# A decoder block's second stage: row transposes, router product and both halves of the routing one step later

## What is computed

```python
x = x + self_attention(layernorm(x))                 # 16 heads, ALiBi, causal
x = x + cross_attention(layernorm(x), ctx, mask)     # 8 heads of 64, 750 context rows of 384
h = layernorm(x)
scores = softmax(h @ w_router)                       # 8 experts
weights, experts = top_k(scores, 2)
slot = position of the token among those of its expert, in order of the tokens
x = x + sum_k weights[k] * expert_k(h) + bias        # 896 slots for each expert
```

## Time and profile before

| | |
|---|---|
| median of three runs | 3380.05 us |
| the profiled execution | 3391.78 us, of which 3390.1 us from the first to the last instruction |
| mean granted clock of TensorE | 0.951 |
| busy over the span | PE 91%, DVE 49%, ACT 40%, POOL 22% |
| first stage | from 0 to about 840 us |
| second stage | from about 840 to 1980 us, a batch in the loop in about 71 us |
| third stage | from about 1980 us to the end |

### The profile page before, as it was taken

One profiled execution on the slowest core, in us unless ns is written; L12 is line 12 of the kernel. 1 busy time (PEld: TensorE's weight loads), 2 busy tenths in 40 slices (PEclk: granted clock), 3 DMA queues, 4 the chain that ended last, 5 costly groups with the idle time before them and its releaser, 6 DMA issues. The chain is left out here.

```text
span 3390.1 us, 52927 instructions
## 1 busy us (share of the span) xinstructions
PE 3071.0 (91%) x19340; PEld 2500.3 (74%) x19340; DVE 1669.1 (49%) x3816; ACT 1351.4 (40%) x2297; POOL 732.2 (22%) x564
## 2 busy tenths in 40 slices
PE   5889999865999999999999839999999999999997
PEld 4667777754777777777777628887888788878886
DVE  5888888843555565555555623232223232323232
ACT  5677777743555555555555411111111111111111
POOL 0000000001112222121221123333333333333333
PEclk9889999977999999999999859999999999999999
DMA  2011111114111111111110022222222222222222
GB/s 95 23 34 44 43 43 43 44 50 145 37 37 43 36 51 52 36 37 42 48 54 23 17 70 72 61 83 70 74 61 83 70 74 63 81 72 72 66 78 59
DMA packets 96191, 193.80 MB, mean 57 GB/s; under 512 B 18656, under 2 KB 28640, under 8 KB 94016
## 3 DMA queue, kind: packets, MB, share of 16 engines
q1 hardware_dynamic: 80912, 160.78, 15.6%
q0 software_dynamic: 15152, 31.26, 4.4%
HBM read 144.19 MB, written 47.82 MB: 57 GB/s over the span
## 5 line engine op out<-in xcount | busy, mean ns | idle before, releaser
L1619 DVE CAST f_hh<-f_hf 128x448 fp32r<-128x448 f32 x256 | 116.8, 456 | 893.2 <-ACT f_hf L1643 860.5
L1643 ACT ACTIVATE f_hf<-f_h 128x448 f32<-128x448 f32 x256 | 139.6, 545 | 1016.0 <-PE f_h L1679 983.2
L1566 POOL TENSOR_TENSOR f_w1l<-f_raw,f_w1h 128x512 fp32r<-128x512 f32 x130 | 183.4, 1411 | 829.2 <-DVE f_w1h L1601 829.1
L1695 PE MATMUL f_y<-f_w2h,f_hh 128*128 128x512 f32 x896 | 357.9, 399 | 0.0
L1695 PE MATMUL f_y<-f_w2h,f_hl 128*128 128x512 f32 x896 | 354.0, 395 | 0.0
L1695 PE MATMUL f_y<-f_w2l,f_hh 128*128 128x512 f32 x896 | 352.3, 393 | 0.0
L1266 ACT ACTIVATE c_s_sb<-c_s_sb,c_nmx 112x750 f32<-112x750 f32 x256 | 236.0, 922 | 188.9 <-DVE c_nmx L1095 186.5
L1679 PE MATMUL f_h<-f_xTh,f_w1h 128*128 128x448 f32 x1024 | 261.8, 378 | 32.3 <-ACT f_hf L1643 16.8
L1258 ACT COPY c_pT<-c_psum 125x672 f32<-125x672 f32 x256 | 184.7, 722 | 241.1 <-PE c_psum L1359 237.4
L1359 PEld LDWEIGHTS c_psum<-c_ident,c_s_sb 112*125 112x125 f32 x1536 | 198.2, 194 | 90.2 <-issue 84.5
L1679 PE MATMUL f_h<-f_xTl,f_w1h 128*128 128x448 f32 x1024 | 256.1, 373 | 0.0
(11 more groups left out here) (243 smaller groups left out, 5725.5 us busy)
## 6 DMA issues: line engine op xcount, KB each, us to landing
f_raw<-in_w SPq DMA_DIRECT2D x132, 512.0 KB
c_craw<-in_ctxT SPq DMA_DIRECT2D x16, 1125.0 KB, 5.1
a_x_in<-in_x SPq DMA_DIRECT2D x9, 896.0 KB, 5.7
a_xr<-in_x SPq DMA_DIRECT2D x8, 896.0 KB, 6.0
x_dram<-a_xr SPq DMA_DIRECT2D x8, 896.0 KB, 4.8
q_dram<-a_q SPq DMA_DIRECT2D x32, 224.0 KB, 5.3
c_q<-q_dram SPq DMA_DIRECT2D x16, 448.0 KB, 5.5
c_x<-x_dram SPq DMA_DIRECT2D x16, 448.0 KB, 4.6
```

The lines of the kernel that those rows point to most:

```text
L1566: pool.tensor_tensor(w1s[1][:, n % NSLOT].rearrange("p k c -> p (k c)"), raw1[:, g % 2, n % 2, :], w1s[0][:, n % NSLOT].rearrange("p k c - ...
L1619: dve.tensor_copy(hs[0][:, l % 2, c * HC:c * HC + HC], hf[:, c, :]).then_inc(h_hi, 1)
L1643: act.activation(hf[:, c, :], H[:, 0:HC], ACT.Gelu_apprx_tanh).then_inc(free, 1)
L1695: mm = pe.matmul(Y[t][:], hs[a][:, l % 2, 128 * t:128 * t + 128], w2s[b][:, l % NSLOT, :], start=j == 0 and q == 0, stop=j == FB - 1 and q ...
```

## The change

Five things move one step on in each batch: XT(0) from step 7 to 8, XT(1) from 8 to 9, RT from 10 to 11 (in the last slot, behind K(2,0)), DVE's two halves of the routing from 11 to 12 and from 14 to 15, and ACT's small exponential from 11 to 12. PRE goes from the end of step 13 to the first slot of step 14, behind the scores and ahead of the transposes of that step. No instruction is added or taken away.

```diff
--- before.py
+++ after.py
@@ -817,9 +817,9 @@
         RT, PRE = ("RT", 0, 0), ("PRE", 0, 0)
 
         PLAN = {0: ([], [K(3, 1)], []), 1: ([], [PV(3)], [V(1, 0)]), 2: ([], [V(1, 1)], []), 3: ([], [V(1, 2), OUT(0)], []),
-                4: ([], [OUT(1)], []), 5: ([], [PV(0)], []), 6: ([], [K(0, 0)], []), 7: ([], [K(0, 1)], [XT(0)]),
-                8: ([], [K(1, 0)], [XT(1)]), 9: ([], [PV(1)], []), 10: ([], [V(0, 0)], [RT]), 11: ([K(1, 1)], [K(2, 0)], []),
-                12: ([], [V(0, 1)], []), 13: ([], [PV(2)], [PRE]), 14: ([], [V(0, 2)], []), 15: ([K(2, 1)], [K(3, 0)], [])}
+                4: ([], [OUT(1)], []), 5: ([], [PV(0)], []), 6: ([], [K(0, 0)], []), 7: ([], [K(0, 1)], []),
+                8: ([], [K(1, 0)], [XT(0)]), 9: ([], [PV(1)], [XT(1)]), 10: ([], [V(0, 0)], []), 11: ([K(1, 1)], [K(2, 0)], [RT]),
+                12: ([], [V(0, 1)], []), 13: ([], [PV(2)], []), 14: ([PRE], [V(0, 2)], []), 15: ([K(2, 1)], [K(3, 0)], [])}
         LATE = (K(3, 1), V(1, 0), V(1, 1), V(1, 2))
         START = [K(0, 0), K(0, 1), K(1, 0), K(1, 1), K(2, 0), V(0, 0), V(0, 1), V(0, 2), K(2, 1), K(3, 0)]
 
@@ -1199,9 +1199,9 @@
                     residual(i, kind, s // 4)
                 elif s == 6:
                     layernorm(i)
-                elif s == 11:
+                elif s == 12:
                     routing(i, kind, 0)
-                elif s == 14:
+                elif s == 15:
                     routing(i, kind, 1)
 
             mask_of(0)
```

## The result

The change makes the kernel slower: 3476.86 us in the median of six runs (3471.33 to 3484.63) against 3381.09 us for the kernel before on the same chips, a ratio of 1.0282 with a 95% interval of 1.0269 to 1.0295. The forecast was 3461 us and the range 3437 to 3495. Of the 95.8 us that were added, the forecast had 81.

What follows compares the result with a forecast made beforehand. PE was taken to bound the second stage, except in a stall ended by DVE's masking. Terms 5.5 + 13.7 + 46.6 - 4 = 62 us, plus 20 for the clock, made 82: 3461 us from the median of 3380.05, range 3437 to 3495.

Steps and rivals of the forecast that it cites:

- What bounds the stage: Second stage: PE is busy but for one stall of 1.23 and 0.91 us a batch, ended by DVE's masking before S(8).
- Term A: Transposes and router product: XT(0), moved out of the stall behind S(8), costs 0.39 us a batch; 5.5 us.
- Term B: Routing's first half in step 12: DVE's masking delays S(14) from +7.85 to +8.83 after S(12); 13.7 us.
- Term C: PRE and routing's second half: K(2,1) waits 3.0 us for PRE's bank; S(0) comes 3.33 us later a batch, 46.6 us.
- Rival 3: PRE's bank doesn't hold K(2,1), being given back ahead of head-half 1's masking; 20 us added, 3400 us; chance 0.07.
- Term D: PE's waits for ACT's copy, 4.3 us over the second stage, should mostly go: -4 us.
- The clock: Drops of the granted clock behind stalls: 11 at K(2,1) of 1.6 us, 2 more at step 8 of 1.2; 20 us.
- Rival 1: DVE's waits as forecast, but clock drops stay as many as they are: 62 us added, 3442 us; chance 0.22.
- Rival 2: The clock drops behind all three stalls in every batch: 113 us added, 3493 us; chance 0.12.
- The prediction's last step: Adding 82 us to the profiled 3391.8 us gave 3473 us; from the median of 3380.05 us, 3461 us.
- rival 4: Faster: the wait for the layernorm ahead of S(8), priced at 17.2 us, goes for good, 3363 us; chance 0.04.
- rival 5: Nothing that shows: the moved pieces are small and cancel, within 0.3% of 3380 us (10 us); chance 0.03.

Runs made afterwards that it cites:

- e9: As e3, with the layernorm's root left in step 6 and the scaling of the rows moved behind the masking of step 7: 3392.45 us, ratio 1.0029.
- e12: As e10, with the last three instructions of the layernorm's root also moved behind the masking, into step 7: 3356.51 us, ratio 0.9916.
- e10: As e9, with POOL's two additions on x1 held until DVE has scaled head-halves 9 and 11: 3365.52 us, ratio 0.9954.
- e5: Kernel before with only RT moved to step 11 and the routing's first half and ACT's small exponential to step 12: 3398.05 us, ratio 1.0057.
- e3: Kernel before with only XT(0) and XT(1) moved, to steps 8 and 9: 3396.40 us, ratio 1.0043.
- e2: Changed kernel with only the routing second half's first two instructions (reading PRE, giving its bank back) in step 14, the rest in 15: 3401.60 us, ratio 1.0057.
- e7: The kernel before, unchanged, run once more for a second profile: 3384.00 us, ratio 1.0003.
- e1: Changed kernel with the whole second half of the routing back in step 14: 3399.77 us, ratio 1.0053 to the kernel before.
- e6: Kernel before with only PRE moved to step 14 and the second half of the routing to step 15: 3442.15 us, ratio 1.0172.
- e11: Kernel before with only POOL's two waits of e10 added: 3378.42 us, ratio 0.9990.

## Why the prediction was right, and where it was off

- **What bounds the stage.** PE, but for DVE's masking at S(8). Right, and shown by e9 and e12, which move work from ahead of the masking to behind it and shorten S(6) to S(8) by 0.97 and 1.70 us.
- **Term A**, the transposes. Forecast 0.39 us a batch, measured 8.30 - 7.77 = 0.53 from S(8) to S(10) less 0.10 from S(10) to S(12), so 0.43. The total is near, the places were not quite right: XT(0) takes over XT(1)'s place at no cost, and it is XT(1), now behind PV(1), that costs 0.53 us (1389.49 to 1390.02 above), where I had written "nothing"; the 0.10 is saved by RT, for which I had also written "nothing". e10, which moves XT but not RT, has 8.30 in every batch and still 9.77 from S(10) to S(12); e5, which moves RT, has 9.66. That the stall itself stays is shown by e3 (S(6) to S(8) 8.86).
- **Term B**, the first half. Forecast S(12) to S(14) 8.83, measured 8.84. The chain held link by link: DVE goes on at +4.61 (1404.31 - 1399.70), forecast +4.62; the negation is at +8.74, forecast +8.81. Shown by e5.
- **Term C**, PRE and the second half. Forecast +3.33 a batch, measured 11.60 - 8.43 = 3.17 in the four batches without a drop: K(2,1) starts at +7.65 (1416.19 - 1408.54), forecast +7.75, and waits 2.87 us, forecast 3.0. That the giving back of PRE's bank and nothing else holds K(2,1) is shown by e2, where the wait goes with those two instructions alone. Rival 3 falls.
- **Term D**, the waits for ACT's copy: forecast -4 us, measured nothing: the second profile of the kernel before (e7) doesn't have them, and no other kernel's profile shows them in this place. This was the step that failed: it took a row that varies between executions of one kernel for a property of the kernel.
- **The clock.** Forecast 20 us: 11 drops at K(2,1) of 1.6 us and 2 more at S(8) of 1.2. Measured at K(2,1): 10 drops of 1.5, 15 us. At S(8): the drops take 14 x (9.96 - 8.30) = 23 us after and 14 x (8.81 - 7.77) = 15 us in e7, so 9 us more where I had 2.4. The number of drops was near (10 at either place, forecast 11); the size at S(8) wasn't. A drop there costs 1.1 us or 2.5, and I had priced one from the cheaper kind, though the profile of the kernel before has one batch with the dearer (10.34 against 7.77). That the number came near is partly luck: I had no rule for it, and a stall of the same 2.72 us has a drop behind it in 10 batches of 14 in the changed kernel, 4 in e1, 5 in e2 and 14 in e3. Rival 1, no further loss by the clock, falls. It was also what the Trainium skill's advice on idle gaps would have said ("TensorE: Matmul & The Clock Gate", section "Why this matters for your kernels"); the trace disagrees, with drops in 10 of 14 batches behind waits of 2.72 and of 2.87 us. Rival 2, a drop behind all three stalls, falls too: none in 14 follows the wait of 1.28 us.
- **Rivals 4 and 5** had 0.07 together. e3 shows what the wait for the layernorm was worth once the transposes stepped out of it: nothing. So rival 4 falls, and rival 5 by the 95.8 us.

The sum that the two profiled executions show, 6 + 14 + 44 + 0 + 24 = 88 us, is 6 above my 82 (4 at term D, 4 at the clock, and 2 less at term C). The other 8 us between 88 and 96 are the distance of those executions from their medians. The prediction's last step is also 1 us low: 3391.8 + 82 is 3474, not 3473, and so 3462, not 3461.

## What to carry to other kernels

Where engines work in a fixed order and share buffers in turn, look for each moved piece at who gets its buffer next: here one small instruction, put behind 3 us of other work, held the bank of a unit that had nothing to do with it, and cost 57 of 96 us there and 77 in all, with the clock. A unit that runs inside a stall is free; moved out of it, it costs its full time, and the stall stays as long as what sets its end stays. To shorten such a stall, move work on the releasing engine behind the instruction that is waited for, and look at what else that releases: the same move lost 11 us with a neighbour set free at the wrong moment and won 17 with the neighbour held back.

## What the runs showed of the hardware

The granted clock in a batch of the changed kernel. The windows lie around the stall before S(8), whose scores start at 1068.44, and around the wait at K(2,1), which starts at 1105.44; columns as in the earlier trace rows (window, its length, busy us of PE, its weight loads, DVE, ACT and POOL with the number of instructions, granted clock, DMA share, GB/s):

```profile
1065.70:1068.40 2.70, 0.03 (x1) 0.00 (x0) 2.54 (x6) 0.00 (x0) 1.42 (x1) 0.92 0.20 60
1068.40:1070.40 2.00, 1.96 (x6) 1.08 (x8) 0.15 (x1) 1.37 (x3) 1.34 (x1) 0.50 0.46 149
1070.40:1072.40 2.00, 2.00 (x9) 1.18 (x6) 1.02 (x3) 0.00 (x0) 0.00 (x0) 0.50 0.78 218
1072.40:1074.40 2.00, 2.00 (x9) 2.00 (x8) 0.76 (x3) 1.54 (x4) 0.00 (x0) 0.50 0.76 240
1074.40:1076.40 2.00, 2.00 (x17) 1.86 (x17) 1.71 (x5) 1.47 (x5) 1.31 (x1) 0.90 0.00 1
...
1102.50:1105.40 2.90, 0.05 (x1) 0.00 (x0) 2.09 (x8) 1.08 (x3) 0.00 (x0) 1.00 0.00 0
1105.40:1107.40 2.00, 1.96 (x6) 1.96 (x7) 1.59 (x10) 0.00 (x0) 0.00 (x0) 0.53 0.00 0
1107.40:1109.40 2.00, 2.00 (x11) 2.00 (x11) 0.28 (x2) 0.47 (x1) 0.80 (x1) 0.61 0.00 0
1109.40:1111.00 1.60, 1.60 (x12) 1.36 (x10) 0.00 (x0) 1.52 (x3) 1.09 (x2) 1.00 0.02 1
```

After a stall of 2.7 us the clock fell to 1.2 GHz (0.50) while PE was still idle (the mean of 0.92 in the first window is 1.00 up to 1068.00 and 0.50 in the last 0.4 us) and stayed there for over 6 us, through the scores, the transposes and most of K(1,0), although PE was busy all the time; S(8) to S(10) took 10.84 us. After a stall of 2.9 us in the same batch it fell as PE began again and came back within 4 us. The same stall of 2.72 us before S(8) costs nothing (4 batches of the changed kernel, 10 of e1), 1.1 to 1.2 us (13 batches of e3) or 2.4 to 2.5 us (9 batches of the changed kernel). What decides between them was not tried, but two patterns say that it isn't the stall alone. In e3 the stall and the 71.8 us from batch to batch are alike, and yet the scores behind the stall take 1.52, 1.55, 1.60, 1.66 us and so on up to 2.51 from the second batch of the loop to the last: the clock falls a little earlier against the stall in each batch. And two stalls in one batch share their drops: in the changed kernel the four batches without a drop at S(8) are the four without one at K(2,1), while in e6 the six batches with a drop of 2.5 us at S(8) have none at K(2,1), and the seven without a drop at S(8) all have one there. So the drops behind one stall can't be counted by looking at that stall, and mending one stall (e1) can change what another costs.

I had not expected either that short waits close together can have drops behind them: two waits of 1.23 and 0.91 us with 0.57 us of transposes between them had drops behind them in 9 of 14 batches in both profiles of the kernel before (4 in e5, 7 in e6 and 7 in e11). One of 1.75 us in one piece had none in e10 and one in e9, where the scores of one batch take 2.74 us.
